# Graph layers on one core: the index columns of both edge loops staged by SyncE's queue (SBUF to SBUF) in place of copies on GpSimd

## Reference, cut to what matters

```
# layer 0
basis    = products of two hat functions of edge_attr_2        # 9 per edge
messages = einsum('ek,ei,kio->eo', basis, x[src], weight)      # 32 per edge
x = layernorm(x + segment_sum(messages, dst) / max(degree, 1) + x @ root_w.T + root_b)
# layer 1
R   = relu(edge_weight[:, None] @ w1 + b1) @ w2 + b2           # 384 per edge
Y   = spherical_harmonics(edge_attr_3)
msg = contraction of R, Y and features[src]                    # 32 per edge
x = layernorm(x + segment_sum(msg, dst))
```

## Time and profile before

| | us |
|---|---|
| median of three runs (lowest, highest) | 12081.6 (12078.4, 12100.4) |
| span of the profiled execution, first to last instruction | 11991.0 |
| what the runs hold around that span (runs less span) | 87.4 to 109.4 |
| first edge loop: first and last spread begin at | 122.8 and 4799.5 |
| second edge loop: first and last gather of `idx_a` begin at | 5087.9 and 11868.7 |
| POOL busy, 80 to 4805 us | 3613.4 of 4725 |
| DVE busy, 5200 to 11800 us | 5629.0 of 6600 |

### The profile page before, as it was taken

How to read it: one execution, slowest core, us unless ns; L and a number is a source line. 1 busy time by engine, 2 the same in 40 slices (tenths; PEclk the granted TensorE clock), 3 DMA queues, 4 the chain that set the end, 5 groups by cost and what they waited for, 6 DMA issues and landing times. The chain is left out here.

```text
span 11991.0 us, 122458 instructions
## 1 busy us (share of the span) xinstructions
PE 7745.6 (65%) x35701; PEld 5552.3 (46%) x35701; DVE 7532.1 (63%) x14033; ACT 817.6 (7%) x1907; POOL 6643.3 (55%) x6757
## 2 busy tenths in 40 slices
PE   5777777777777777455555555555555555555555
PEld 5777777777777777322222222222222222222223
DVE  4333333333333333588888888888888888888887
ACT  0000000000000000000000000000000000000000
POOL 5777777777777777044444444444444444444443
PEclk5555555555555555577777777777777777777776
DMA  1000000000000000011111111111111111111111
GB/s 36 11 11 11 11 11 11 11 11 11 11 11 11 11 11 11 37 39 36 39 36 39 36 39 36 39 36 39 37 39 37 39 37 38 37 38 37 38 37 29
DMA packets 251980, 327.74 MB, mean 27 GB/s; under 512 B 110894, under 2 KB 160959, under 8 KB 251087
## 3 DMA queue, kind: packets, MB, share of 16 engines
q0 software_dynamic: 200000, 205.20, 9.1%
q1 hardware_dynamic: 51962, 122.31, 3.2%
HBM read 320.67 MB, written 6.40 MB: 27 GB/s over the span
## 5 line engine op out<-in xcount | busy, mean ns | idle before, releaser
L411 PE MATMUL sums_ps<-hot,spread 128*96 128x64 f32 (+1 forms) x18750 | 3183.6, 370 | 1075.5 <-DVE spread L361 1075.5
L411 PEld LDWEIGHTS sums_ps<-hot,spread 128*96 128x96 f32 (+1 forms) x18750 | 3068.2, 281 | 1221.4 <-DVE spread L361 650.7
L361 DVE TENSOR_TENSOR spread<-basis,rows 128x1440 f32<-128x1440 f32 x625 | 1039.8, 1664 | 3215.1 <-DMA rows<-in_x,idx_a 1902.4
L754 PE MATMUL radial_x<-edge_t,hidden 128*128 128x384 f32 x3750 | 1916.7, 664 | 1211.3 <-DVE edge_t L856 1121.4
L282 POOL DMA_INDIRECT rows<-table_dram,idx_a x1875 | 1772.3, 945 | 1484.6 <-DVE prods_y L856 889.6
L282 POOL DMA_INDIRECT rows<-in_x,idx_a x1875 | 2140.3, 1141 | 634.2 <-issue 533.3
L754 PE MATMUL radial_y<-edge_t,hidden 128*128 128x384 f32 x2500 | 1377.7, 689 | 1509.5 <-DVE prods_y L856 1509.5
L754 PEld LDWEIGHTS radial_x<-edge_t,hidden 128*128 128x128 f32 x3750 | 886.1, 252 | 1856.0 <-issue 920.2
L282 POOL DMA_INDIRECT rows<-in_x,idx_b x1250 | 1422.4, 1138 | 443.7 <-issue 342.8
L282 POOL DMA_INDIRECT rows<-table_dram,idx_b x1250 | 1188.9, 951 | 766.7 <-DVE prods_y L856 363.0
L754 PEld LDWEIGHTS radial_y<-edge_t,hidden 128*128 128x128 f32 x2500 | 555.7, 246 | 2273.4 <-DVE prods_y L856 2014.4
(11 more groups left out here) (121 smaller groups left out, 3794.7 us busy)
## 6 DMA issues: line engine op xcount, KB each, us to landing
dist<-in_edge_weight SPq DMA_DIRECT2D x625, 160.0 KB, 3.2
rows<-in_x,idx_a POOLq DMA_INDIRECT x1875, 2.4
rows<-table_dram,idx_a POOLq DMA_INDIRECT x1875, 2.5
rows<-in_x,idx_b POOLq DMA_INDIRECT x1250, 2.4
rows<-table_dram,idx_b POOLq DMA_INDIRECT x1250, 2.5
acc<-in_edge_attr SPq DMA_DIRECT2D x1, 4687.5 KB
table_dram<-edge_t SPq DMA_DIRECT2D x1, 4687.5 KB
acc<-in_edge_attr SPq DMA_DIRECT2D x1, 3125.0 KB
```

Of the source, the lines that this page charges most:

```text
L361: dve.tensor_tensor(spread[s][:, :, 0:K].rearrange("e t (k c) -> e t k c", c=C), basis[s][:, :, :].unsqueeze(3).to_broadcast([P, G, 9, C]) ...
L411: last = pe.matmul(sums_ps[s][0:m, c * WINDOW:(c + 1) * WINDOW], spread[s][:, j, c * CH:c * CH + m], hot[s][:, j, :], start=(j == 0 and c ...
L754: last = pe.matmul(radial[h][:, j, 0:R], hidden[s][:, (j0 + j) * P:(j0 + j + 1) * P], w2p[:, :], start=True, stop=True)
```

## The change

The two copies on POOL go, with their semaphore. SP loads `idx_a` and `idx_b` from `src_t` by two DMAs per iteration (128x15 and 128x10 int32, 7.5 and 5 KB). POOL waits for the landing instead, once at unit 0 and once at unit 3. `idx_a` of the next iteration is loaded when the rows of units 0 to 2 have landed. `idx_b` is loaded when all units of the iteration before have been consumed. In the second loop SP's index loads stand in the same queue program as the `dist` loads: `idx_b` behind the second, `idx_a` behind the fifth. The last iteration is written out, since it loads the first columns again.

```diff
+def load_indices(sp, keep, idx, idx_landed, half, i):
+    first, n = ((0, 3 * G), (3 * G, 2 * G))[half]
+    sp.dma_start(idx[half][:, :], keep["src_t"][:, bass.ds(i * (U * G) + first, n)]).then_inc(idx_landed[half], 16)
...
-    def gather(g, i, u):
+    def gather(g, u):
         pool.wait_ge(rows_used, freed(g, u))
         if u in (0, 3):
-            n = 3 if u == 0 else 2
-            pool.tensor_copy(idx[u // 3][:, 0:n * G], src_t[:, bass.ds(i * (U * G) + u * G, n * G)]).then_inc(idx_ready, 1)
-            pool.wait_ge(idx_ready, g * 2 + (1 + u // 3))
+            pool.wait_ge(idx_landed[u // 3], (g + 1) * 16)
         pool.sem_inc(gathers_begun, 1)
...
@@ spline_edges, block.sync
+            passes = load_passes(sp, keep)
+            load_indices(sp, keep, idx, idx_landed, 0, 0)
+            with sp.Fori(0, passes) as p:
+                def body(i, after):
+                    g = p * B + i
+                    sp.wait_ge(spread_ready, g * U + CREDIT)
+                    load_indices(sp, keep, idx, idx_landed, 1, i)
+                    for u in range(3):
+                        sp.wait_ge(rows_landed[SLOT[u]], filled(g, u, 16 * G))
+                    load_indices(sp, keep, idx, idx_landed, 0, after)
...
@@ tensor_edges, block.sync
                 def body(i, after):
                     g = p * B + i
+                    load_dist(g, i, 0)
+                    load_dist(g, i, 1)
+                    sp.wait_ge(prods_ready[1], g * U + CREDIT)
+                    load_indices(sp, keep, idx, idx_landed, 1, i)
+                    for u in (2, 3, 4):
+                        load_dist(g, i, u)
+                    for u in range(3):
+                        sp.wait_ge(rows_landed[SLOT[u]], filled(g, u, 16 * G))
+                    load_indices(sp, keep, idx, idx_landed, 0, after)
```

More of the change, by code:

```diff
@@ L289, in pool_gathers @@
             for u in range(U):
-                gather(g, i, u)
+                gather(g, u)
 def spline_edges(nc, keep, x, weight0):
@@ L316, in spline_edges @@
         msg_ps = [ctx.enter_context(nc.psum_tensor(f"msg_ps{n}", [P, 512], F32)) for n in range(SLOTS)]
-        gathers_begun = sem("l0_gathers_begun")
-        step, wk_landed, wk_ready, idx_ready = sem("l0_step"), sem("wk_landed"), sem("wk_ready"), sem("l0_idx_ready")
+        step, wk_landed, wk_ready = sem("l0_step"), sem("wk_landed"), sem("wk_ready")
+        gathers_begun, indices_done = sem("l0_gathers_begun"), sem("l0_indices_done")
+        idx_landed = [sem("l0_idx_a_landed"), sem("l0_idx_b_landed")]
         rows_landed = [sem(f"l0_rows_landed{n}") for n in range(SLOTS)]
@@ L328, in _ @@
                 sp.dma_start(wk[0:CH, c, 0:C], weight0[3 * c:3 * c + 3].rearrange("k i o -> (k i) o")).then_inc(wk_landed, 16)
+            passes = load_passes(sp, keep)
[8 more added lines that the diff above has]
+                    load_indices(sp, keep, idx, idx_landed, 0, after)
+                with sp.Fori(0, B - 1) as i:
+                    body(i, i + 1)
+                body(B - 1, 0)
+            sp.wait_ge(idx_landed[0], passes * (B * 16) + 16)
+            sp.sem_inc(indices_done, 1)
         @block.gpsimd
         def _(pool):
-            pool_gathers(nc, pool, keep, x, idx, rows, C, idx_ready, gathers_begun, spread_ready, rows_landed)
+            pool_gathers(nc, pool, keep, x, idx, rows, C, idx_landed, gathers_begun, spread_ready, rows_landed)
         @block.vector
@@ L709, in _, with load_dist, body @@
             passes = load_passes(sp, keep)
+            load_indices(sp, keep, idx, idx_landed, 0, 0)
+            def load_dist(g, i, u):
+                sp.wait_ge(hidden_ready, freed(g, u))
+                part = edge_weight[bass.ds(i * (U * G * P) + u * G * P, G * P)]
+                sp.dma_start(dist[SLOT[u]][:, :], part.rearrange("(o e) -> o e", o=1).to_broadcast([HID, G * P])
+                             ).then_inc(dist_landed[SLOT[u]], 16)
             with sp.Fori(0, passes) as p:
-                with sp.Fori(0, B) as i:
+                def body(i, after):
                     g = p * B + i
[L713 to L718, removed]
+                    load_dist(g, i, 0)
[7 more added lines that the diff above has]
+                    load_indices(sp, keep, idx, idx_landed, 0, after)
+                with sp.Fori(0, B - 1) as i:
+                    body(i, i + 1)
+                body(B - 1, 0)
+            sp.wait_ge(idx_landed[0], passes * (B * 16) + 16)
+            sp.sem_inc(indices_done, 1)
         @block.gpsimd
         def _(pool):
-            pool_gathers(nc, pool, keep, table_dram, idx, rows, ROW, idx_ready, gathers_begun, prods_ready[1], rows_landed)
+            pool_gathers(nc, pool, keep, table_dram, idx, rows, ROW, idx_landed, gathers_begun, prods_ready[1], rows_landed)
         @block.scalar
```

8 lines of the change are left out of this document (4 added, 4 removed).

## The result

| | us |
|---|---|
| before, four runs beside the change: median (lowest, highest) | 12090.99 (12078.36, 12107.45) |
| after, four runs: median (lowest, highest) | 12403.98 (12382.59, 12429.56) |
| ratio, 95% interval | 1.0257 [1.0238, 1.0276] |
| span of the profiled execution of after, and its own time | 12427.8, 12429.56 |

The account below looks back on a forecast made before the run. Gathers were taken to bound the first loop wholly and the second at one place. 96 + 45 = 141 us off the 11991.0 us span, plus 90.6 us untouched, gave 11941 us, range 11880 to 12040.

Parts of the forecast that it names:

- Part 2: Second loop, POOL's index copy of unit 0 gone: 0.36 us less wait in each of 125 iterations, 45 us gained.
- Part 3: Second loop, POOL's index copy of unit 3 gone: nothing gained, as dots waits only for rows of `idx_a`.
- Part 4: SP's index loads, 250 in each loop, land at least 8 us before their use: cost 0.
- Part 5: Second loop, three `dist` loads now leave SP together, with a margin of 3 us and more: cost 0.
- gaps: Time from a unit's last gather's end to its spread or dots; first loop: over 1.51 us the next second gather escapes.
- that rival: Second loop, unit 1: `dist` loads delay dots by 1.6 us per iteration, net 59 us slower, 12141 us; chance 0.05.
- Part 1: First loop, POOL's copies gone: more second gathers escape behind third and fifth units, 96 us gained, -/+ 60.
- The rival of the pages' whole-instruction rule: First loop: an escaping gather holds the spread back, gaining only 0.3 us; 12013 us, within a shared chance of 0.03.
- escape: First loop: a unit's second gather starts just before the spread and isn't held to its end, worth 1.22 us.
- 79 escapes x 1.22 = 96 us gained: First loop: 64 fifth-unit and 15 third-unit gaps exceed the limit, each shortening a step by 1.22 us.
- The runs hold 90.6 us more than the span, none of it touched: Whole kernel: runs take 12081.6 us against the profile's span of 11991.0; the difference stays and is added to the forecast.

Follow-up runs that it names:

- e4: Before, with SP also loading the index columns in the first loop to spare tiles nobody reads: 12072.86 us, 1.0001 of before.
- e12: The change unaltered, run on chip E against before: 11828.74 us, ratio 0.9877.
- e15: Before, unaltered, run on chip E for its trace: 11977.45 us.
- e8: After, with PE summing two of a unit's five tiles in the first loop (6 matmuls instead of 15), chip D: 11843.44 us, 0.9872 of before.
- e9: After, with the first-loop matmuls of the middle three tiles 16 columns wide instead of 64, same number, chip D: 11870.08 us, one run.
- e1: Before, with the change in the second loop only, chip B: 12042.66 us, 0.9963 of before.
- e3: Before, with ACT instead of POOL making the first loop's index copies, no SP index loads, chip B: 12297.93 us, 1.0166 of before.
- e7: After, with PE's first-loop program written out for four iterations, chip C: 12201.4 us, 1.0113 of before.
- e17: After, with PE summing two of a unit's five tiles in the first loop, chip F: 12003.92 us, 0.9923 of before.
- e19: After, with each first-loop spread waiting until PE has summed the unit before, chip F: 12923.51 us, 1.0684 of before.
- e5: After, with filler copies to spare tiles on POOL at units 0 and 3 of the first loop, chip C: 12020.61 us, 0.9971 of before.
- e6: After, with a filler copy to a spare tile on POOL at unit 0 only of the first loop, chip C: 12088.64 us, 1.0016 of before.
- e18: After, with the first-loop matmuls of the middle three tiles 16 columns wide instead of 64, chip F: 12415.76 us, 1.0263 of before.
- e10: Before, with the change in the second loop only and PE's first-loop program written out for four iterations, chip D: 11946.94 us, 0.9961 of before.

## Why the prediction was wrong

**The steps that held.** *Part 2*: product to first gather at unit 0 fell from 1.24 us (8024.91 to 8026.15) to 0.88. In after the product ends at 8383.39:

```profile
8382.39 1.00 DVE L895 TENSOR_TENSOR prods_y<-radial_y,rows 128x384 f32<-128x384 f32 x2
8384.27 0.94 POOL L283 DMA_INDIRECT rows<-table_dram,idx_a  x1 [12.65 <-DVE prods_y L895]
...
8391.85 0.28 DVE L863 TENSOR_TENSOR dots<-rows,edge_t 128x120 f32<-128x120 f32 x1 [3.77 <-DMA rows<-table_dram,idx_a]
```

DVE idles 3.77 us where it idled 4.29, 3.9 forecast. 0.36 us times 125 are 45; the loop is 42 to 54 us shorter in the traces of all six chips. *Part 3*: product to first gather at unit 3 fell by 0.42 us, product to dots stayed 13.97: nothing gained. *Part 4*: a load of 5 KB is moved within 1.4 us of its issue (2508.17 to 2509.52) and nobody waits for it; e4 prices 250 of them at nothing. *Part 5*: the gaps of unit 1 in the second loop are 1.71 us before and 1.70 after (medians), so the three `dist` loads cost nothing and that rival falls.

*Part 1*, where nothing pauses (e12 against e15, counts of steps under 7 us): behind fifth units 89 of 124 are short, 0 before, 64 forecast. Behind third units 4, 15 forecast. Second units, which the change doesn't touch, give 99 against 82 on that chip. In all 230 against 116, at 1.22 us some 139, and the loop is 136 us shorter (4658.8 to 4522.5) for 96 forecast, within the 96 ± 60. Mean step 7.25, forecast 7.34. Only 93 of the 114 new short steps stand where a copy was; the other 21 come from a drift of the gaps, which part 1 had only in its bounds. On chip D the two kernels with less work for PE gain just 70 to 76 us in this loop (e8 and e9: 4590.5 and 4596.9 against 4666.9). The counts were off because the gap of buffer 1 was 1.53 to 1.545 us there, a few hundredths over the 1.51 that decides. The rival of the pages' whole-instruction rule, 0.3 us an escape, falls with these 136 us, and the spread beside the escaping gather above took 1.73. With the 48 of the second loop that makes 184, the difference of the two spans (11975.6 - 11792.2 = 183.4). By medians it is 157, against 141.

**The step that failed** is part 1's "79 escapes x 1.22 = 96 us gained", and with it that no part has a term for PE: each rival too took the gathers for the bound. In after PE bounds the first loop, and the loop is 485 us longer, not 96 shorter. On chips A, B, C and F an escape comes with a late release. This shows before the long stretches of pauses set in. Take only units behind three whose releases were in time and whose steps were even (6 to 8.2 us), in the six traces e1 and e3 to e7. At 268 of 268 short steps the release of the unit ahead of the step is late (by 0.8 us at least, typically 3), at 0 of 896 long steps it is. (Without the condition on the steps before, 318 of 446 and 56 of 1146.) In e17 it is 39 of 48 and 3 of 89; in the other traces of these chips too few units are undisturbed, and in e19 the step itself waits for the release. In the nine traces of the other kind 1386 short steps bring no late release. The gather escapes as the spread begins, some 7 us before PE ends that unit's sums, so the escape isn't the effect of the late release. One such place, behind a second unit, in the unaltered first loop of e1:

```profile
347.59 1.73 DVE L390 TENSOR_TENSOR spread<-basis,rows 128x1440 f32<-128x1440 f32 x1 [5.44 <-DMA rows<-in_x,idx_a]
347.63 0.94 POOL L311 DMA_INDIRECT rows<-in_x,idx_a  x1 [0.30 <-issue]
...
349.45 5.09 PE L440 MATMUL sums_ps<-hot,spread 128*97 128x64 f32 x30 [1.94 <-DVE spread L390]
...
354.06 1.66 DVE L390 TENSOR_TENSOR spread<-basis,rows 128x1440 f32<-128x1440 f32 x1 [4.10 <-DMA rows<-in_x,idx_a]
...
357.77 0.27 ACT L483 ACTIVATE sums<-sums_ps 96x128 f32<-96x128 f32 x1 [10.55 <-remote]
```

PE ends the sums at 354.54 and ACT starts at 357.77. So what the change set out to buy, more escapes, is what brings the trouble on these chips, and before has some too, behind second units. Over six units from an escape on, the loop gains 1.0 to 1.3 us on the other chips against a long step; in these six traces the mean difference lies between 0.6 us gained and 4.5 lost, known to 0.4 to 1.5 us.

**The sign that was misread** is "The runs hold 90.6 us more than the span, none of it touched". A run holds 1.8 us more than its span, not 90.6 (12429.56 against 12427.8). The shown profile of before was one of an execution without pauses, and its listed runs were slower ones: 12066 to 12093 us is what before takes on chips B, C and F, 11986 to 11997 on D and E. Those 90 us were the first loop, as the traces of e1 and e4 on slower chips show, which have before's code on POOL and PE there (4766 and 4759 us against 4677); before itself was not traced on such a chip. I had the number in hand and read it as an overhead outside the program. The forecast of 11941 would have come out the same, since 141 us came off the runs either way. But it was a second behaviour of the loop that the change works on, with 0 in the trace I priced from.

**How the loss grows.** DVE's lead of two units hides most of a late release while steps are 7.5 us. Then a stalled unit is followed by spreads 2.2 us apart (2541.48 and 2543.70 behind the place shown above), whose sums PE must run back to back, and the next stretch follows. That this feeds the loss is read from the order of events; e19, meant to show it, had no pause and was slower still. Pauses go by the copies left on POOL in this loop: two (e1, e4, e5) 144 to 184 pauses, one (e6) 353, none (e3, e7, after) 552 to 1302, and in this order on chip B (e1, e3) and on chip C (e4, e5, e6, e7) taken alone. e5 and e6, which differ in one filler, show that the missing copy lets them in.

**What stays open** is why a chip pauses. Shown: SP's loads (e3, e4), the width of the matmuls (e18), PE's branch alone (e7) and the clock are not it, and less work for PE shrinks it (e17). One thing separates the two kinds of chip without exception: all eleven traces with 46,000 to 57,000 semaphore updates have late releases, and all nine with 126,000 to 133,000 have none, for one and the same kernel too. On chip F nearly two thirds of the updates are missing, in the second loop too. Timed runs come with spans as the profiled one does, so I take them to have been recorded likewise. I take it as the likeliest story that the recording itself holds PE back. "NOTIFIC — the notification-queue block" of the Trainium skill, § Overflow: three behaviours, one of which stalls the engine, says that this block's inner pipeline holds its producer back and doesn't drop a record, and that its stalls would mean that it had throttled an engine; its § Block-level registers (shared by all 10 queues) has the runtime clear that hold for the semaphore source. That would give what the traces show: no PE record is missing (35701 in both), PE stands still, and the width of its matmuls doesn't matter. No run here shows it: no kernel was timed without a recording, and e19, late at a lower rate of instructions, isn't explained in detail. Missing records alone don't lengthen a loop either: the second takes 6749 to 6755 us on chip F with two thirds of them gone, and, for the changed second loop, 6750 to 6754 on D and E with all. Note also that with so many updates lost the word "remote" names a missing record; only the start times prove lateness.

## What to carry to other kernels

Before pricing a change, ask why the runs and the span differ: a gap of 90 us that later traces show as 1.8 is not overhead, it is a loop that ran otherwise than in the profile. Here the removal of stalls on one engine raised the rate at which the next engine's instructions come, and the case for such a change needs that engine's slack in the slowest execution at hand, not in the cleanest. And try the winner on more than one chip: this change is worth -1.2% or +2.7% by the chip alone; the second loop's part alone is worth -0.4% on both kinds (e1, e10) and is what I would keep.

## What the runs showed of the hardware

- Chips differ: before takes 11986 to 11997 us on two and 12066 to 12093 on three others. In the traces the difference lies in one loop (4659 to 4677 us in before's, 4759 and 4766 in those of e4 and e1).
- On the slower chips (e1, e3 to e7) each of 268 short steps behind undisturbed units came with a late signal from PE, and none of 896 long ones; on the others none of 1386 short ones.
- PE can stand still between two weight loads that wait for nothing, for up to 2.6 us at a time and 1161 us in all, and its completions can reach ACT and DVE up to 22 and 20 us late (after).
- A SBUF-to-SBUF load of 128 pieces of 40 bytes moves in 0.21 us (2509.31 to 2509.52), 1.1 us behind its issue, 0.49 us of SP's queue.
- In e12's first loop none of 215 gathers that began from 0.3 us ahead of a spread's start to 0.04 us behind it was held, and all of 390 that began 0.05 to 0.9 us behind were (0.94 us at 0.04 us in the place shown, 2.41 us at 0.07 us elsewhere): the limit is that sharp. The spread beside a gather that just escapes takes 1.73 us instead of 1.66.
